# Banded attention in pairs of steps, projections three units ahead, its last superblock written out, and the closing stage folded into the expert stage

## What is computed

```python
x = x + attn_a(layernorm(x))   # 16 heads of 64, rotary, banded
x = x + ffn(layernorm(x))      # 8 experts, the best 2 per token
x = x + attn_b(layernorm(x))   # one head of 128, upper triangle
x = x + ffn(layernorm(x))
```

```python
q = _apply_rope(proj(Wq, bq)); k = _apply_rope(proj(Wk, bk)); v = proj(Wv, bv)
kcat = [block before, own block]          # blocks of W = 128 tokens
scores = einsum('bhnqd,bhnkd->bhnqk', qb, kcat) * scale      # 128 x 256
band = (kj >= qi) & (kj <= qi + W)
attn = softmax(where(valid, scores, -1e30))
ctx = einsum('bhnqk,bhnkd->bhnqd', attn, vcat)
return merged @ Wo.T + bo
```

## Time and profile before

| | |
|---|---|
| timed | 1553.63 us median of 3 (1550.43 to 2271.89) |
| profiled execution | 1557.52 us, its span 1555.8 us |
| granted TensorE clock, mean | 0.911 |
| PE busy | 1285.8 us (83%) |
| DVE busy | 1052.4 us (68%) |
| ACT busy | 905.6 us (58%) |
| POOL busy | 778.7 us (50%) |
| HBM traffic | 91.89 MB, mean 59 GB/s |

### The profile page before, as it was taken

How to read it: one execution, slowest core, us unless ns; L and a number is a source line. 1 busy time by engine, 2 the same in 40 slices (tenths; PEclk the granted TensorE clock), 3 DMA queues, 4 the chain that set the end, 5 groups by cost and what they waited for, 6 DMA issues and landing times. The chain is left out here.

```text
span 1555.8 us, 34583 instructions
## 1 busy us (share of the span) xinstructions
PE 1285.8 (83%) x9684; PEld 1011.7 (65%) x9684; DVE 1052.4 (68%) x3673; ACT 905.6 (58%) x2301; POOL 778.7 (50%) x812
## 2 busy tenths in 40 slices
PE   3999999999999999999963888809978885288890
PEld 2677766766776666766743888805765665288890
DVE  7566877878777776877754555566886788355563
ACT  2677768777776776767642444406765664144450
POOL 3566676685866768567562444500022422435451
PEclk9899999999999999999985999959998998599996
DMA  8999990000000000000013122130000000121215
GB/s 255 210 207 207 208 167 8 4 12 1 15 0 6 10 0 15 0 7 8 0 56 108 56 60 59 45 108 1 1 14 15 25 16 16 45 58 57 62 54 162
DMA packets 129396, 91.89 MB, mean 59 GB/s; under 512 B 9115, under 2 KB 122030, under 8 KB 128992
## 3 DMA queue, kind: packets, MB, share of 16 engines
q1 hardware_dynamic: 118080, 71.84, 21.6%
q0 software_dynamic: 9248, 16.94, 3.3%
q10 hardware_dynamic: 1920, 1.60, 0.3%
HBM read 30.86 MB, written 61.64 MB: 59 GB/s over the span
## 5 line engine op out<-in xcount | busy, mean ns | idle before, releaser
L905 DVE CUSTOM_DVE_ANT_0 sc<-ps,mask 128x256 f32<-128x256 f32 x518 | 199.2, 421 | 159.4 <-PE ps L720 137.1
L827 ACT ACTIVATE sc<-sc,mx 128x256 f32<-128x256 f32 x516 | 256.9, 501 | 38.8 <-DVE mx L905 38.2
L1055 POOL TENSOR_TENSOR rot<-rot,sin 128x512 f32<-128x512 f32 x132 | 183.6, 1391 | 185.9 <-DVE rot L914 185.9
L1202 POOL DMA_INDIRECT yt<-yo,xt x160 | 160.4, 1002 | 197.9 <-DVE yo L1302 169.4
L534 POOL DMA_INDIRECT xg<-r_xw,r_slot x128 | 126.6, 989 | 170.0 <-DVE r_slot L511 137.9
L835 ACT COPY pT<-pt 128x512 f32<-128x512 f32 x257 | 150.1, 584 | 104.0 <-PE pt L730 95.7
L720 PE MATMUL ps<-K,Q 64*128 64x256 f32 x1036 | 193.3, 436 | 14.7 <-DVE mx L905 14.7
L1262 ACT ACTIVATE hT<-ph,b 128x256 f32<-128x256 f32 x320 | 125.4, 475 | 87.0 <-PE ph L1225 87.0
L730 PE MATMUL pt<-ident,sc 128*128 128x128 f32 x1028 | 170.7, 289 | 1.8 <-ACT sc L827 1.6
L743 PE MATMUL po<-pT,V 128*64 128x128 f32 x2048 | 170.7, 288 | 0.0
L730 PEld LDWEIGHTS pt<-ident,sc 128*128 128x128 f32 x1028 | 109.3, 142 | 86.6 <-issue 58.5
(11 more groups left out here) (235 smaller groups left out, 2730.3 us busy)
## 6 DMA issues: line engine op xcount, KB each, us to landing
xg<-zeros SPq DMA_DIRECT2D x76, 520.0 KB, 9.9
xt<-xg SPq DMA_DIRECT2D x80, 130.0 KB, 2.1
got<-yt SPq DMA_DIRECT2D x32, 256.0 KB, 4.4
yt<-yo,xt POOLq DMA_INDIRECT x160, 2.3
xg<-r_xw,r_slot POOLq DMA_INDIRECT x128, 2.3
w<-in_w SPq DMA_DIRECT2D x1, 2048.0 KB, 8.1
out_x<-x SPq DMA_DIRECT2D x8, 256.0 KB, 4.3
x<-in_hidden SPq DMA_DIRECT2D x6, 256.0 KB, 8.2
```

The source lines that it names most:

```text
L827: nc.scalar.activation(sc[:, b, h, :], sc[:, b, h, :], ACT.Exp, scale=-1.0, bias=mx[:, b, h:h + 1], accum_out=ls[:, c % 2, b, h:h + 1]).th ...
L905: nc.vector.tensor_tensor_reduce(sc[:, b, h, :], ps[:, h, 0:2 * P], (mask0 if b == 0 else mask)[:, :], -float(HD) ** -0.5, 3e38, ALU.add, ...
L1055: nc.gpsimd.tensor_tensor(rot[:, which, :], rot[:, which, :], s.sin[:, pos(sb)], ALU.mult).then_inc(S["pool"], 1)
L1202: nc.gpsimd.indirect_dma_start(out=s.yt, out_offset=bass.IndirectOffsetOnAxis(ap=xt[:, k, r, HID:HID + 1].bitcast(U32), axis=0), in_=yo[:, ...
```

## The change

- Scores, transposes and values of two steps stand together. A unit is now two halves j = 0 and 1. PE in half 0: scores of a pair four steps ahead, `project_q`, transposes of a pair two ahead, `project_k`, values of the pair. In half 1: scores, `project_v`, transposes, `project_out`, `turn_sums`, values. `ps` now holds two steps, and PE signals the pair's scores once (by 2).
- Projections run three units ahead (`AHEAD` = 3), so the prologue projects three units.
- ACT and DVE follow in a new order (below); `times_cos` of K moves ahead of the next maxima, `keep_v` behind them.
- The routing no longer borrows `ps` and `pt` but the idle half of `po` (`spare`), at new places: `root` and `normalise` both end half 0 of chunk 2, `exponentials` and `order` half 0 of chunk 4, `accumulate` half 0 of chunk 5. POOL scatters two tiles in chunk 6 and two in chunk 7.
- The loop covers six superblocks; the last one has a body of its own, which leaves out the projections and scores past the end.
- `last_stage` goes; its fetch, add and store stand at the end of `expert_stage` 3, behind SP's own wait for the scattered rows.

```diff
+        AHEAD = 3
...
+            return u, u + AHEAD, (c + AHEAD) % CHUNKS, (sb if c + AHEAD < CHUNKS else sb + 1)
...
-            def scores(c, b, u, G, first=False):
+            def scores(c, j, u, G, first=False):
...
+                for b in (2 * j, 2 * j + 1):
+                    for h in range(2):
+                        if not first and b == 2 * j:
+                            pe.wait_ge(S["max"], START + 2 * G - 1 + h)
+                        r = slice(h * HD, (h + 1) * HD)
+                        ins = nc.tensor.matmul(ps[:, h, bass.ts(b % 2, 2 * P)], Q[r, c % QBUF, b * P:(b + 1) * P],
+                                               K[r, c, b * P:(b + 2) * P], start=True, stop=True)
+                ins.then_inc(S["s"], 2)
...
+                    for j in range(2):
+                        G = SB_TILES * u + 2 * j
+                        if not past_end(G + 4):
+                            scores((c + 1) % CHUNKS, j, u + 1, G + 4)
+                        if not ends(sb, c):
...
+                            if j == 0:
+                                project_q(v, vc, vsb)
                             else:
+                                project_v(v, vc)
+                        if not past_end(G + 2):
+                            for b in range(2):
+                                transposes((2 * j + 2 + b) % SB_TILES, G + 2 + b)
+                        if j == 0 and not ends(sb, c):
                             project_k(v, vc, vsb)
+                        if j == 1:
                             project_out(u - 1, (c - 1) % CHUNKS, sb)
+                            turn_sums(u, ends(sb, c))
...
+                        for b in range(2):
+                            values(c, 2 * j + b, u, G + b)
...
+                        if j == 0 and not ends(sb, c):
+                            read_q(v, vc)
...
+                            probabilities((c + 1) % CHUNKS, 2 * j, G + 4)
...
+                            read_pt((2 * j + 2) % SB_TILES, G + 2)
+                        if j == 0 and not ends(sb, c):
+                            read_k(v, vc)
...
+                            probabilities((c + 1) % CHUNKS, 2 * j + 1, G + 5)
...
+                            read_pt((2 * j + 3) % SB_TILES, G + 3)
...
+                        if j == 1:
                             read_sums(u)
...
+            with act.Fori(0, NSB - 2) as i:
                 turn(i + 1, True)
+            turn(NSB - 1, True)
...
+            if result is not None:
+                for k in range(STEP):
+                    sp.wait_ge(put[k], 32 * (nth + 1) * ROUNDS)
+                fetch_outputs(sp, s, got)
```

More of the change, by code:

```diff
@@ L770, in _ @@
             pe.wait_ge(S["xl"], START + 1)
-            for v in range(2):
+            for v in range(AHEAD):
                 project_q(v, v, 0, head=True)
@@ L776, in _ @@
                 project_v(v, v)
-            for b in range(3):
-                scores(0, b, 0, b, first=(b == 0))
-            transposes(0, 0, first=True)
+            for j in range(2):
+                scores(0, j, 0, 2 * j, first=(j == 0))
+            for b in range(2):
+                transposes(b, b, first=True)
             def turn(sb, routed):
@@ L860, in _ @@
             high_x(0)
-            for v in range(2):
+            for v in range(AHEAD):
                 read_q(v, v, v0=(v == 0))
                 read_k(v, v, v0=(v == 0))
-            probabilities(0, 0, 0)
-            probabilities(0, 1, 1)
-            read_pt(0, 0, first=True)
+            for b in range(SB_TILES):
+                probabilities(0, b, b)
+                if b == 1:
+                    read_pt(0, 0, first=True)
+                    read_pt(1, 1, first=True)
             def turn(sb, routed):
@@ L1082, in unit @@
                 if spreads:
-                    spread(v - 2, (c - 2) % CHUNKS)
+                    spread(v - AHEAD, (c - AHEAD) % CHUNKS)
                 rotate(v, c, sb, 1)
             low_x(0)
-            for v in range(2):
+            for v in range(AHEAD):
                 unit(v, v, 0)
@@ L1138, in expert_stage @@
         S = s.signals[f"experts{tag}"]
+        if result is not None:
+            got = m.sb("got", [P, TOPK, TILES, P])
+            tokens = result.rearrange("b (t p) d -> p (b t) d", p=P)
+            summed = s.signals["last"]["sum"]
         load, put, nth = s.load, s.put, tag // 2
@@ L1193, in _ @@
             rounds(sp, turn)
+            if result is not None:
+                for k in range(STEP):
+                    sp.wait_ge(put[k], 32 * (nth + 1) * ROUNDS)
+                fetch_outputs(sp, s, got)
+                for i in range(NSB):
+                    sp.wait_ge(summed, START + i + 1)
+                    r = slice(i * SB_TILES, (i + 1) * SB_TILES)
+                    sp.dma_start(tokens[:, r, :], s.x[:, r, :]).then_inc(s.s_out, 16)
+                sp.wait_ge(s.s_out, 16 * NSB)
         @block.gpsimd
@@ L1330, in _ @@
             keep(GROUPS - 1, GROUPS - 1, expert(dve, GROUPS - 1))
+            if result is not None:
+                ch = Chain(dve, s.signals["last"]["chain"])
+                for i in range(NSB):
+                    combine(nc, ch, s, got, i, 2)
+                    dve.sem_inc(summed, 1)
 def full_stage(nc, sems, s):
@@ L1749, in bass_hybrid @@
         full_stage(nc, m, s)
[L1750 to L1777 removed]
+        expert_stage(nc, m, 3, s, out)
 def kernel(**inputs):
```

212 lines of the change are left out of this document (92 added, 120 removed).

## The result

The changed kernel takes 1676.55 us, median of four runs (1675.56 to 1678.46), against 1553.22 us for the kernel before, run beside it: a ratio of 1.0802 [1.0781, 1.0823], 123 us slower. One of the four executions of the kernel before took 2271.89 us and is left out of the ratio. The profiled execution has a span of 1674.2 us where before had 1555.8. The granted clock is the same on average, 0.909 against 0.911.

What follows compares the result with a forecast made beforehand. PE's list bounds the attention before, a ring of waits through bank pj after; ring +68.4, routing +26.4, last units -10.6, prologue +6, last stage -5 make +85.2 on 1557.5, 1642.7 profiled, 1639 median; range 1612 to 1672.

Steps and rivals of the forecast that it cites:

- rival A: The forecast itself: attention units paced by the ring at 11.7 to 12.4 us; range 1612 to 1672, chance 0.66.
- the ring: Attention: reads and writes of bank pj waiting in turn across PE, ACT and DVE; 12.00 us a unit against 10.86, +68.4.
- the routing: Routing pieces woven into seven superblocks: 11.2 us each against 7.6, in full where they stand in the ring; +26.4.
- the last three units: End of attention, without Q, K, V and finally scores: 22 us together instead of 32.6, -10.6.
- the prologue: Before the attention's units: projecting a third unit adds 6 us, from the 5.9 between first and second Q.
- the end of the kernel: Folded last stage, last scatter to first fetch: 5 of 9.15 us saved, bounds 0 and 7.
- PE's list: PE's own work in an attention unit: pairing saves 0.92 us, leaving 9.9 instead of 10.86.
- e): DVE's link of the ring, from K's shuffle through product, maxima and keep_v to PE's sums: 3.36 us.
- the upper bound of 12.4: Upper limit for the ring's unit time, if POOL's work stretches DVE's instructions in e).
- Rival B: Attention: the ring, and the clock falls in ordinary units too; one in three paying 2.95 adds 59, 1698; chance 0.12.
- C: Attention: PE stays the bound at 9.9 us a unit, 1486 us in all; chance 0.08.
- D: Attention: the ring without DVE's part, 11.45 us a unit, and the routing at 6 us; 1569 in all; chance 0.14.

Runs made afterwards that it cites:

- number 9: The change with four pT slots, V's add ahead of the maxima, three routing pieces moved and the sums copied early: 1507.00 us, ratio 0.9693 to the kernel before.
- Number 2: The change with one move, DVE's keep_v ahead of the four maxima of half 1: 1606.82 us, ratio 1.0326 to the kernel before.
- number 3: The change with pT holding four steps instead of two, no order altered: 1614.55 us, ratio 1.0375 to the kernel before.
- number 5: The change with accumulate moved from ahead of the maxima of half 1 to the start of chunk 5: 1655.74 us, ratio 1.0660 to the kernel before.
- number 1: The change with ACT's copy of the sums moved ahead of the half's first copy of pT: 1668.86 us, ratio 1.0724 to the kernel before.
- number 4: The kernel before with only last_stage folded into the last expert stage: 1551.71 us against 1559.58, ratio 0.9956.
- number 7: The change with pT of four steps and keep_v ahead of the maxima: 1597.79 us, ratio 1.0287 to the kernel before.
- number 10: The change with pT kept at two steps, sums copied early, V's add early and three routing pieces moved: 1518.60 us, ratio 0.9771 to the kernel before.
- number 6: The change with accumulate at chunk 5's start, normalise a half after root, exponentials and order in DVE's wait for K: 1611.76 us, ratio 1.0377 to the kernel before.

## Why the prediction was right, and where its terms were off

The forecast of 1639 us was 37.6 low and inside its range, and its mechanism, rival A, is the one the trace shows. Measured less forecast, in the profiled execution: the ring +21.6, the routing +12.1, the last three units +0.4, the prologue +4.9, the end of the kernel -5.7, together 33. The other 4.5 are the step from the profiled execution to the median: 3.9 were taken off, and here the median lies 0.6 above. That the errors partly cancel is luck.

**PE's list** was put at 9.9 us. Where PE hardly waits, in superblock 0 of number 9, eight units take 81.8 us with PE busy 81.5, so the list is 10.2. Paired scores stand 1.07 us before what follows and values 1.02 (828.42 to 829.44), as predicted; the paired transposes take 0.87 to 0.94 instead of 0.82, and V 0.99 instead of 0.90. The saving of the pairs is real, and number 9 turns it into time.

**The ring** was put at 12.00 and is 12.36, term by term as in the table above. The 0.36 are mostly the stretched product of e) (+0.3), which the upper bound of 12.4 had named; e) had been priced by the row of Q's product instead of K's. Over the 60 units that is 60 x (12.36 - 10.86) = +90.0 instead of +68.4. Numbers 2 and 3 each cut it at a different place, and both shorten the plain unit, to 11.36 and to 10.1 to 10.7.

**The routing** was +26.4 in the sum. Counted as there (all of the routing before in the first 60 units), it came to 833.1 - (737.2 - 32.6) - 90.0 = +38.5. The total hides errors of opposite sign. `root` and `normalise` were put at 4.4 and the clock at 2.9 more, 7.3: that unit takes 17.04, only 4.7 above a plain one, clock and all. The term that was mis-sized most is `accumulate`, "four of 0.164 with hand-overs: +0.8". It cost 17.24 - 12.36 = 4.9, clock included; number 5 shows that place, not work, made it so. I had read its duration from one row, in a place where POOL happened to be idle. The forecast of what the profile would show had one unit of 16 us or more, and there are two. The kernel before showed the stretching in the rows beside it, which I did not use; groups of DVE instructions by line, 150 to 700 us, of the kernel before:

```profile
L408 DVE TENSOR_SCALAR r_mean<-r_tmp 128x4 f32<-128x4 f32 x6 | 7.4, 1235 | 0.2
L480 DVE TENSOR_TENSOR r_hot<-iota,r_tf 128x32 f32<-128x32 f32 x6 | 7.1, 1182 | 0.2
...
L482 DVE TENSOR_TENSOR r_hot<-iota,r_tf 128x32 f32<-128x32 f32 x6 | 4.9, 810 | 0.0
```

and the same lines over 150 to 850 us of the changed kernel:

```profile
L480 DVE TENSOR_TENSOR r_hot<-iota,r_tf 128x32 f32<-128x32 f32 x6 | 1.2, 192 | 0.2
...
L408 DVE TENSOR_SCALAR r_mean<-r_tmp 128x4 f32<-128x4 f32 x6 | 1.2, 200 | 0.2
L482 DVE TENSOR_TENSOR r_hot<-iota,r_tf 128x32 f32<-128x32 f32 x6 | 1.1, 183 | 0.0
```

The same small instruction takes 0.2 us or 1.2, by what POOL does at that moment: in the kernel before all six of line 480 and all six of line 408 end 0.02 to 0.05 us after an instruction of POOL with two inputs, and all 24 of line 488 stand where POOL does nothing. Before, it was others that met POOL's work, under the cover of a busy PE. The remaining units of the superblock cost 0.8 (chunk 3), 1.7 (chunk 4, where `order` was put at 1.5) and 1.4 (chunk 6, with the copy of `mask0`, put at 0.4).

**The clock.** In both units of the change with an idle piece of 4.5 us the mean clock is 0.90; in its plain units with 1.18 and 0.79 us idle it is 1.00, and over the 63 units it is 0.97. Rival B (ordinary units slow down too) did not happen in the change. In numbers 1 and 3 something like it did, as the table above shows, and there my expectations had nothing for it.

**The last three units** were put at 22 and take 22.40.

**The prologue** was put at +6 and came to +10.9. The passage that a third unit adds was priced at the 5.9 us from the first unit's Q to the second's in the kernel before, where the mean clock was 0.85. In the change it is the passage from the second's Q to the third's, and it ran at low clock throughout:

```profile
37.33:45.07 7.74, 5.37 (x14) 3.45 (x15) 4.03 (x7) 1.37 (x2) 7.05 (x7) 0.50 1.23 212
```

7.74 us at a clock of 0.50, the lower of the two levels. The rest, 3.1, is the first Q's later start (30.86, was 29.77), the first unit's 6.5 us instead of 5.9, and 20.9 us instead of 19.4 from the first scores to the first copy of the sums.

**The end** was put at -5, all of it for the folded stage, and came to -10.7. Between the last scatter and the first fetch 7.0 us went, in the change and alone in number 4. But other pieces of the closing stages are longer in both traces than in the one of the kernel before: the last expert stage's scatters take 157.2 us from first to last instead of 154.0, and from the first fetch to the end it is 23.4 to 23.5 instead of 22.2. With one trace of the kernel before, I cannot say how much of that is the fold's; timed, number 4 gains 3 to 11. What the forecast left out is the start of `tail_stage`. DVE's first instruction there comes 11.47 us after unit 63's copy in the kernel before, 4.29 in the change; first the row of the kernel before, then that of the change:

```profile
810.62 0.87 DVE L402 BATCH_NORM_STATS2 r_stats<-x 128x6 f32<-128x128 f32 x4 [8.12 <-PEq L645]
```

```profile
932.58 0.87 DVE L402 BATCH_NORM_STATS2 r_stats<-x 128x6 f32<-128x128 f32 x4 [0.63 <-PEq L645]
```

Before, POOL's four scatters of the last unit ended at 805.60, 6.5 us after that copy, and all engines then met at the end of the stage. In the body written out for the last superblock POOL's last scatter ends at 926.92, 1.4 us ahead of the copy. These 7.2 us were in no term of the sum. Number 4, which has the fold and not this body, starts its tail at 11.47 like the kernel before; that the scatters are what the meeting waited for is my reading of the rows.

**The other rivals.** C, PE stays the bound, needed the sums', K's and V's reads early, which the change does not have. Number 9 does, and there PE is nearly the bound. D took the ring without DVE's part at 11.45 and the routing at 6 us a superblock, 1569 in all. Number 2 is the first half of that, plain units of 11.35 to 11.39, but its superblocks take 12.9 beyond eight of them, and the kernel 1606.82.

My expectations of the runs were worse than the prediction in one way: in numbers 1, 3 and 7 I subtracted a wait that was seen, though it stood beside a second chain almost as long, and took the clock as given.

## What to carry to other kernels

When instructions are grouped in pairs to save changes on the busiest engine, follow one buffer that several stages take in turn through the lists of the other engines: each read of it that now stands behind a wait for the end of the pair is a link of a ring, and here the place of two such reads and of the routing's pieces decided between 8% slower and 2% faster (number 10; with the slots 3%, number 9). A small instruction's duration is only good for the place where it was read; look at the same engine's other small rows for a stretched one before pricing a move, and put such work where the engine next door is idle. A wait that stands beside a second chain cannot be subtracted by itself: of three moves of order, alone, one gave 8.9 us a superblock, one 10.3 and one 0.3, and the last gave 2.1 once the others were in. Read the granted clock of each unit before calling a move worthless.

## What the hardware showed that I had not expected

In the rows shown, DVE's instructions with two SBUF inputs that ran beside POOL's ended with them or a fixed time after. The product with the cosines, 0.67 us by itself, ended 0.55 us after the end of POOL's addition in all three units shown (321.50 to 322.05, 831.63 to 832.18 and 488.92 to 489.47), and four additions of 128 by 8 numbers took 3.26 us instead of 4 x 0.168. One of the stretched groups of the kernel before, line 408 at 1235 ns, reads a single tile; it too ends within 0.03 us after POOL's addition for K, all six times, and no run here tells why.

The longest wait of PE does not tell by itself whether the clock falls. In the change, waits of 4.5 us came with a mean of 0.90 in their units, and waits of 2.2 and 2.5 us with 1.00. But the unit of chunk 6 ran at 0.88 in number 6 and at 0.80 in number 1, where its longest wait was 1.9 us, and one unit of the kernel before ran at 0.79 with a longest wait of 1.42.
